# Adaptive-norm block with sampled attention and a top-2 expert layer on one core: the last expert folded out of the masks, the first norm's squares moved, expert products split

## The reference

```
h = layernorm(x) * (1 + ca) + sa
x = x + ga * attn(h)          # sampled positions, 33 samples a token, 8 heads
h = layernorm(x) * (1 + cb) + sb
logits = h @ router_w.T + router_b           # 8 experts
mask = one_hot(top 2 of the logits).sum()    # 8 numbers a token: two ones, six zeros
out = sum over e of mask[e] * (expert_w[e] h + expert_b[e])
x = x + gb * out
```

## Time and profile before

| | |
|---|---|
| time, median of 3 runs | 294.6 us (293.69 to 295.03) |
| the profiled execution's own time | 293.6 us |
| its span, first to last instruction | 291.8 us |
| PE busy | 262.0 us, 90% |
| DVE busy | 262.0 us, 90% |
| ACT busy | 226.9 us, 78% |
| POOL busy | 62.7 us, 21% |
| DMA queues | 12.93 MB, mean 44 GB/s |
| granted TensorE clock | 1.00 in every turn, 0.998 over the span |

### The profile page before, as it was taken

The page is one execution under the profiler, slowest core; times in us unless marked ns, Lnnn a source line. Parts: engine busy times, 40 slices in busy tenths (PEclk is TensorE's granted clock), DMA queues, the critical chain, the costliest instruction groups (busy, mean ns, idle before and its releaser), DMA issues.

```text
span 291.8 us, 5429 instructions
## 1 busy us (share of the span) xinstructions
PE 262.0 (90%) x1867; PEld 181.0 (62%) x1876; DVE 262.0 (90%) x543; ACT 226.9 (78%) x641; POOL 62.7 (21%) x59
## 2 busy tenths in 40 slices
PE   8899886899798999889998999889999989899995
PEld 3544642665486487647784569548884768476664
DVE  7989989998979999999999899989999999982671
ACT  4885899699897998699869989799779767655310
POOL 4103101800451023502080026202340300010100
PEclk9999999999999999999999999999999999999999
DMA  6560000020004000320014000500041004100101
GB/s 179 161 160 0 0 0 0 3 74 1 1 2 163 2 1 0 97 86 3 0 29 155 0 0 2 183 2 1 2 130 53 1 0 125 60 2 0 36 2 54
DMA packets 12011, 12.93 MB, mean 44 GB/s; under 512 B 1021, under 2 KB 10960, under 8 KB 11216
## 3 DMA queue, kind: packets, MB, share of 16 engines
q1 hardware_dynamic: 11540, 12.19, 13.9%
q10 hardware_dynamic: 444, 0.40, 0.5%
HBM read 10.44 MB, written 2.15 MB: 43 GB/s over the span
## 4 chain that ended last, share of the span: by engine, by line
ACT 31%; PE 26%; DVE 18%; POOL 12%; issue 11%; ACTq 0%; DVEq 0%; POOLq 0%
PE pE L1136 9%; ACT A L507 8%; DVE AT L835 8%; POOL rs L327 8%; ACT xn L405 4%; ACT c L490 4%; POOL nm L329 4%; PE pE L985 3%; ACT xn L371 3%; DVE T L802 3%; PE pY L1136 3%; PE pR L1028 2%; ACT hT L428 2%; ACT y L529 2%; DVE hm L902 2%
## 5 line engine op out<-in xcount | busy, mean ns | idle before, releaser
L802 DVE COPY_PREDICATED T<-mask,T 128x1472 f32<-128x1472 int16 (+9 forms) x54 | 76.2, 1411 | 0.5
L835 DVE TENSOR_TENSOR AT<-T,c 128x2064 f32<-128x2064 f32 x32 | 72.3, 2300 | 0.0
L1136 PE MATMUL pE<-hm,late 128*128 128x256 f32 x224 | 52.6, 386 | 0.0
L1136 PEld LDWEIGHTS pE<-hm,late 128*128 128x128 f32 x224 | 41.2, 190 | 6.6
L507 ACT ACTIVATE A<-pT 128x512 f32<-128x512 f32 x64 | 34.7, 600 | 12.6 <-PE pT L1051 12.5
L327 POOL TENSOR_TENSOR rs<-ve,mhalf 128x4 f32<-128x4 f32 (+1 forms) x18 | 32.5, 1806 | 44.3 <-DVE ve L715 37.5
L321 POOL TENSOR_SCALAR ve<-sq 128x4 f32<-128x4 f32 (+1 forms) x14 | 7.0, 502 | 162.9 <-ACT xn L371 162.9
L405 ACT ACTIVATE xn<-x,nm,rs 128x128 f32<-128x128 f32 x64 | 26.5, 485 | 16.1 <-POOL nm L329 16.1
L1051 PE MATMUL pT<-first,AT 128*128 128x128 f32 x256 | 34.2, 276 | 4.8 <-DVE AT L845 4.7
L1051 PEld LDWEIGHTS pT<-first,AT 128*128 128x128 f32 x256 | 28.3, 141 | 11.4 <-DVE AT L845 9.9
L507 ACT ACTIVATE A<-pR 128x512 f32<-128x512 f32 x64 | 35.2, 619 | 0.0
(11 more groups left out here) (145 smaller groups left out, 389.2 us busy)
## 6 DMA issues: line engine op xcount, KB each, us to landing
mkb<-mask_rows SPq DMA_DIRECT2D x6, 1024.0 KB, 5.3
x<-in_x SPq DMA_DIRECT2D x7, 256.0 KB, 6.1
out<-x SPq DMA_DIRECT2D x7, 256.0 KB, 5.3
late<-in_late SPq DMA_DIRECT2D x1, 592.0 KB, 3.9
mkb<-mask_rows SPq DMA_DIRECT2D x1, 512.0 KB, 3.6
x<-in_x SPq DMA_DIRECT2D x2, 128.0 KB, 3.7
wmod<-in_wmod ACTq DMA_DIRECT2D x1, 256.0 KB, 3.5
out<-x SPq DMA_DIRECT2D x2, 128.0 KB, 3.2
```

The lines of the kernel that those rows point to most:

```text
L802: nc.vector.copy_predicated(rows[:, :, :, j0:j1], spread(mask[:, k, 0:w, j0:j1], [P, w, H, j1 - j0], 2), rows[:, :, :, j0 + (1 << bit):j1 ...
L835: nc.vector.tensor_tensor(cells_of(bt).rearrange("p h (j r) -> p h j r", r=BLK), spread(T[n % 2][:, bt, 0:H, 0:NB], [P, H, NB, BLK], 3), s ...
L1136: ins = mm(dst, weT[:, e, :], hm[b][:, e, :], start=False, stop=(e == E - 1))
```

## The change

It has five parts.

1. **One masked input fewer.** Since a token's mask entries sum to 2, the expert sum is 2 W7 h plus the sum over e < 7 of mask[e] (We - W7) h. `expert_weights` on DVE rewrites the weights once, in turn 1 (subtract W7 from the other seven, double W7). `masked` makes seven inputs (128x1792 instead of 128x2048), the broadcast rows and the selectors are seven, and in the late units the last quarter has one expert. The biases still use all eight mask rows.
2. **Biases and the eighth expert for the whole unit.** `back_plain` makes one product 2 W7 h (float32, 512 columns for a full unit) and one bias product (bf16, 512 columns) per unit, then seven expert products for each image. `back_plain` does not need the masked inputs.
3. **ACT's order.** `sums1` goes behind `norm2` (for turns from 0 on in front of h2T), and `squares1` in front of `back_moe`.
4. **PE's order.** The second image's experts are parted: five of them, then `back_x2T`, then the last two, then the router product. The four `warm_up` products between `back_x2T` and the router stay in turns 1 and 2 only; turn 1 has 23 instead of 18 before them.
5. **The tail.** DVE does `residual(7)` and `stats2(7)` before `masked(6, 1)`, which also waits until POOL has rs of unit 7. PE has 5 and 6 `warm_up` products around y of unit 7 and parts the experts of units 6 and 7 in another way. `selectors` moves to turn 0.

```
 E = 8
+EM = E - 1
...
-                sp.dma_start(scratch[n % 2][:, 0:w], mkT[0:E, 0:w]).then_inc(d_mk, 16)
+                sp.dma_start(scratch[n % 2][:, 0:w], mkT[0:EM, 0:w]).then_inc(d_mk, 16)
...
                 if i >= 0:
                     run(i, 1, front_hs)
-                run(i, 2, sums1)
                 run(i, 1, front_u)
                 run(i, -1, norm2)
                 if i < 0:
                     run(i, 1, front_hs)
+                run(i, 2, sums1)
                 run(i, -1, back_h2T)
+                run(i, 2, squares1)
                 run(i, -2, back_moe)
-                run(i, 2, squares1)
                 run(i, 0, mid_A, 0)
...
+            def expert_weights():
+                dve.wait_ge(d_late, 32)
+                nc.vector.tensor_tensor(weT[:, 0:EM, :], weT[:, 0:EM, :], spread(weT[:, EM, :], [P, EM, C], 1),
+                                        ALU.subtract).then_inc(v_we, 1)
+                dve.wait_ge(v_we, 1)
+                nc.vector.tensor_scalar(weT[:, EM, :], weT[:, EM, :], 2.0, None, ALU.mult).then_inc(v_we, 1)
...
-                nc.vector.tensor_tensor(hm[b][:, :, :], mkb[n % 2][:, :, b * L:(b + 1) * L],
-                                        spread(own, [P, E, L], 1), ALU.mult).then_inc(v_hm, 1)
+                                        spread(own, [P, EM, L], 1), ALU.mult).then_inc(v_hm, 1)
...
                 run(i, 0, network, range(5, 6))
+                if i == 0:
+                    selectors()
+                elif i == 1:
+                    expert_weights()
                 run(i, 1, line)
...
             set_ends(LAST, 0)
-            masked(LATE - 1, 1)
             residual(LATE)
             stats2(LATE)
+            dve.wait_ge(g_rs2, LATE + 1)
+            masked(LATE - 1, 1)
             route(LATE)
...
+            def back_plain(n):
+                if n == 0:
+                    pe.wait_ge(v_ebp, 8)
+                    pe.wait_ge(v_we, 2)
...
+                pe.wait_ge(a_mk, n + 1)
+                w = tiles(n) * P
+                mm(moe_bank(n)[:, 0:w], weT[:, EM, :], h2T_of(n)[:, 0:w], start=True, stop=False)
+                mm(moe_bank(n)[:, 0:w], ebp[:, :], mkT_of(n)[:, 0:w], start=False, stop=False)
...
                 run(i, -2, back_experts, 0)
-                second(i, -2, back_experts, 1)
+                second(i, -2, back_experts, 1, range(0, 5))
                 if i == 1:
-                    warm_up(18)
+                    warm_up(23)
                 elif i == 2:
                     warm_up(12, pT[0])
                 run(i, -1, back_x2T)
-                if i > 0:
+                second(i, -2, back_experts, 1, range(5, EM))
+                if 0 < i < 3:
                     warm_up(4, pT[0])
                 run(i, -1, back_logits)
```

More of the change, by code:

```diff
@@ L299, in masks @@
                     sp.wait_ge(v_hm, before(n - 1))
[L300 removed]
+                sp.dma_start(mkb[n % 2][:, :, 0:w], spread(scratch[n % 2][:, 0:w], [P, EM, w], 0)).then_inc(d_mkb[n % 2], 16)
             def store(n):
@@ L952, in _ @@
                     gates()
-                    selectors()
             network(LAST, range(0, 1))
@@ L1122, in back_mb @@
                         pe.wait_ge(v_hm, masked_before(before(n) + b - 1) + k + 1)
-                    for a in range(2):
+                    for a in range(min(2, EM - 2 * k)):
                         ins = mm(four_banks(k)[:, a * L:(a + 1) * L], sel[:, 2 * k + a, :], mkT_of(n)[:, b * L:(b + 1) * L],
@@ L1126, in back_mb, with back_experts @@
                     ins.then_inc(t_mb, 1)
-            def back_experts(n, b, own=range(E)):
+            def back_experts(n, b, own=range(EM)):
                 img = before(n) + b
-                dst = moe_bank(n)[:, b * L:(b + 1) * L]
                 if own[0] == 0:
-                    back_biases(n, b, dst)
+                    if b == 0:
+                        back_plain(n)
+                    if n < LATE:
+                        pe.wait_ge(v_hm, img + 1)
                 for e in own:
@@ L1202, in _ @@
             mid_attend(LATE, 1, 1)
+            warm_up(5, pT[0])
             mid_y(LATE)
-            back_experts(LATE - 1, 0)
+            warm_up(6, pT[0])
+            back_experts(LATE - 1, 0, range(0, 2))
             mid_gate(LATE)
+            back_experts(LATE - 1, 0, range(2, EM))
             mid_A(LAST, 0, 0)
@@ L1224, in _ @@
             back_mb(LATE, 1)
-            back_experts(LATE, 0, range(6, E))
+            back_experts(LATE, 0, range(6, EM))
             back_experts(LATE, 1, range(0, 3))
```

56 lines of the change are left out of this document (25 added, 31 removed).

## The result

| | before | after |
|---|---|---|
| median | 294.8 us (293.69 to 295.07, 4 runs) | 287.4 us (287.32 to 287.54, 4 runs) |
| ratio, 95% interval | | 0.9756 [0.973, 0.9782] |
| profiled execution, its span | 293.6 us, 291.8 us | 287.4 us, 285.5 us |
| PE, DVE busy | 262.0, 262.0 us | 258.3, 258.9 us |
| ACT, POOL busy | 226.9, 62.7 us | 227.2, 53.7 us |

Faster by 2.4%. The forecast was 288.8 with a range of 286.8 to 292.3. The spans differ by 6.3 us where the sum said 5.8. The executions of one kernel here differ by up to 3 us, with mean granted clocks from 0.98 to 1.00; in before most lie near 293.4 or near 295, so its median moves by a microsecond between sessions.

A forecast was written before the change was run, and what follows sets the result against it. The prediction took a ring ACT, POOL, ACT, PE, DVE, 1.0 us a turn longer than DVE's own work, as the bound. Savings of 0.2 + 0.3 + 4.2 + 0.6 + 0.5 = 5.8 us gave 288.8 us, range 286.8 to 292.3.

The forecast's parts named there:

- The masks: DVE's masked inputs, two in a turn: 256 fewer elements save 0.28 us each, 0.57 us a turn.
- ACT's order frees rs: Full turns: earlier squares let POOL's rs start at 24.2 to 24.8 us and finish before DVE's products hold it.
- nm is caught: Full turns: DVE's products still hold POOL's nm; residual can start at 11.11 us, waiting 0.17 in place of 1.00.
- Turns 4 to 6: Three full turns, each 1.40 us shorter (31.77 to 30.37): 4.2 us together.
- Turns 0 to 2: First turns, with the weights' rewrite and the router wait: 0.2 us won together, between 0.3 lost and 0.8 won.
- The tail: After the turns: 0.5 us won, 0.2 from an earlier xn and 0.3 on PE; between 1.0 lost and 2.2 won.
- The median: Whole kernel: median taken as 1.0 us above the profiled execution, so 287.8 us became 288.8.
- rs still caught: Rival, chance 0.12: POOL's rs is still held by DVE, residual stays at 12.22 us, only 2.4 us saved: 292.2 us.
- Both POOL operations free: Rival, chance 0.12: POOL's nm also ends before hits, so the 0.17 us wait goes in four turns: 288.2 us.
- The router late: Rival, chance 0.12: sums1 ahead of h2T makes DVE wait before lg, 0.6 us in turns 3 to 6: 291.2 us.
- The clock: Rival, chance 0.05: without four warm products PE's clock falls in the full turns; slower than before, for example 300 us.
- DVE pays for POOL: Rival, chance 0.04: DVE's products wait for POOL's rs, 0.6 us in turns 3 to 6, 2.4 us: 291.2 us.

## Why the prediction was right

- **The masks.** 0.28 a piece in the sum, 0.26 measured (2276 less 2015).
- **ACT's order frees rs.** Right, and it was the main term. With seven masks it took the full turns from 31.80 to 30.28, while the masks had given them nothing without it. It is enough by itself, but in this kernel not needed: PE's order had freed rs too. ve was to start 23.9 behind `set_ends` and started 23.94 behind it (173.08 less 149.14); rs was to start 24.2 to 24.8 behind it and did at 24.49; DVE was to reach `hits` at 25.42, and did at 25.33.
- **nm is caught.** Right: 4.88 us, and `residual` possible at 11.11, found at 11.12.
- **Turns 4 to 6**, 4.2 in the sum, 4.4 measured (1.49, 1.48 and 1.42). The term was short by `lg`: I read "no wait" and took at least 0.5 us of cover. There was none: DVE had lost 0.16 there in each turn (0.40 behind the first image's `set_ends`, 0.24 in the changed kernel), too little for a bracket. The runs with ACT's old order show the same place at its worst, 0.3 to 0.35. That step was wrong, harmlessly, since h2T came 1.8 us earlier (21.02 behind `set_ends` for 22.79) and DVE only 1.5.
- **Turns 0 to 2**: 0.2 in the sum, 0.17 measured. The `lg` wait of turn 2 grew from 1.92 to 2.22 as said of `sums1`.
- **Turn 3**: 0.3 in the sum, 0.41 measured, with a wait of 0.38 ahead of `residual` (0.28 by the sum). **Turn 7**: 0.6, and 0.58.
- **The tail**: 0.5 in the sum, 0.75 measured. xn of unit 7 was to gain 0.2 and gained 0.62 (18.70 behind turn 7's `set_ends` for 19.32); PE's transposes lost 0.95 where 1.1 was said, and ACT's copies end 0.7 later than before and not 1.1 (18.70 for 18.01, which is the earlier trace rows' 263.15 less the 1.31 in its bracket). The sum used that bracket; the words that xn started just when the copies were done passed over it: xn had waited 1.31 for nm. What I didn't see is that nm would be caught by the very product that waits for rs, and that mkT would wait for the last expert product. That wait takes back most of xn's gain: mkT is 0.20 earlier (26.23 behind `set_ends` for 26.43), and from mkT to the end 0.55 is won where the sum had 0.3. So the total of the tail is near its forecast in part by luck.
- **The median**: I added before's 1.0 us over its profiled execution. The changed kernel's runs lie at theirs (287.4), so this 1.0 was too much and makes most of the 1.4 by which the forecast was high.
- **The rivals.** rs still caught: it is what happens with the masks alone (291.8). Both POOL operations free: 288.2 was forecast (288.8 less four times 0.17 is 288.1), and the old ACT order's turns, where nm is held for only 1.60, come near that case, 0.2 less a turn. The router late: not in turns 3 to 6, where `lg` stands 0.24 or 0.25 behind the first image's `set_ends` and has no bracket. The clock: 1.00 in the turns. DVE pays for POOL: not seen; `hits` and the products start on time while rs runs, and the 32 products on AT take 2299 ns on average. Here the run decides against the rule that the prediction weighed from the Trainium skill (SBUF — State Buffer, Who interferes with whom), which has the one issued first block the other. DVE did not pay. On POOL's side the rule fits in part: operations started inside the products waited, but rs with a recorded start ahead of both `hits` and the products was held as well (0.07 and 0.34 ahead, 6.00).
- **PE's order**, costed at nothing, gave nothing (30.28 either way) with ACT's new order. I had not seen that with ACT's old order it frees rs, if by some 10 ns only.

## What to carry to other kernels

When a small operation of POOL sits on the path between two long products of DVE with both inputs in SBUF, its place counts more than its length: find how far ahead of the product it starts, and move what feeds it, before cutting work from the busiest engine. Cutting DVE's work gave nothing (31.80 for 31.77) until that was done. Where two chains end within 0.1 us of each other, undoing either one alone shows no effect, so test the pair. A gain early in a tail can be lost to a wait further on, so compare the distances up to the end. And an idle time without a bracket is not proof of cover: compare distances between the neighbours' starts.
